# The scaled systems of the 32-row inversion kept in two PSUM banks

## What is computed

```python
def step(S, inputs):
    q_t, k_t, v_t, g_t, b_t = inputs
    S = S * jnp.exp(g_t)[..., None, None]
    kv = jnp.einsum('bhk,bhkv->bhv', k_t, S)
    u = b_t[..., None] * (v_t - kv)
    S = S + jnp.einsum('bhk,bhv->bhkv', k_t, u)
    o_t = jnp.einsum('bhk,bhkv->bhv', q_t * scale, S)
    return (S, o_t)
...
up_w = ste_sign(up_weight)
down_w = ste_sign(down_weight)
hidden = jnp.einsum('bsd,hd->bsh', x, up_w) * up_scale
hidden = jax.nn.relu(hidden)
out = jnp.einsum('bsh,dh->bsd', hidden, down_w) * down_scale
```

## Time and profile before

| | |
|---|---|
| time, median of 3 runs | 1524.98 us (1524.01 to 1525.74) |
| the profiled execution, its time | 1525.26 us |
| its span, first to last instruction | 1523.5 us |
| PE busy | 1365.2 us, 90% of the span |
| DVE busy | 1120.9 us, 74% |
| ACT busy | 724.5 us, 48% |
| POOL busy | 517.7 us, 34% |
| granted TensorE clock, mean | 0.975 |
| chain that ended last, DVE L1728 | 3% of the span |
| the same, DVE L1730, L1736, L1747 | 1% each |

### The profile page before, as it was taken

The page is one execution under the profiler, slowest core; times in us unless marked ns, Lnnn a source line. Parts: engine busy times, 40 slices in busy tenths (PEclk is TensorE's granted clock), DMA queues, the critical chain, the costliest instruction groups (busy, mean ns, idle before and its releaser), DMA issues. The chain is left out here.

```text
span 1523.5 us, 24300 instructions
## 1 busy us (share of the span) xinstructions
PE 1365.2 (90%) x8972; PEld 662.7 (43%) x8972; DVE 1120.9 (74%) x1880; ACT 724.5 (48%) x1277; POOL 517.7 (34%) x426
## 2 busy tenths in 40 slices
PE   5878899999999999999798889988899888998887
PEld 2322333333333333333354366543765437654375
DVE  6878977787878777888367956769567785586854
ACT  4664666566655665665554222641225412264121
POOL 2599821022102210222145331452314523155231
PEclk9988999999999999999999999999999999999999
DMA  6420000100010001005502030020310203102121
GB/s 219 159 77 2 6 8 5 34 25 5 10 34 26 5 10 33 26 1 206 190 22 53 6 79 29 15 54 19 66 36 8 53 21 63 36 7 54 27 31 42
DMA packets 79573, 68.51 MB, mean 45 GB/s; under 512 B 45952, under 2 KB 67168, under 8 KB 76896
## 3 DMA queue, kind: packets, MB, share of 16 engines
q1 hardware_dynamic: 79456, 66.96, 14.9%
HBM read 44.87 MB, written 17.87 MB: 41 GB/s over the span
## 5 line engine op out<-in xcount | busy, mean ns | idle before, releaser
L599 DVE TENSOR_REDUCE mS<-bank 128x1 f16<-128x512 f32 x512 | 328.8, 684 | 123.6 <-PE bank L1105 121.7
L917 ACT ACTIVATE probs<-bank 128x512 f16<-128x512 f32 x512 | 277.2, 595 | 163.3 <-PE bank L1112 163.1
L1159 PE MATMUL bank<-rows,both 128*128 128x512 f16 x1024 | 242.9, 380 | 1.1 <-DVE th L628 1.1
L408 POOL TENSOR_TENSOR h<-th,h 128x512 f16<-128x512 f32 x58 | 68.0, 1172 | 235.4 <-ACT h L888 235.4
L2099 PE MATMUL fbank<-both,hid 128*128 128x512 f16 x512 | 122.9, 403 | 24.6 <-DVE hid L1646 24.6
L1159 PEld LDWEIGHTS bank<-rows,both 128*128 128x128 f16 x1024 | 91.4, 98 | 122.3 <-issue 15.8
L2083 PE MATMUL fbank<-rows,both 128*128 128x512 f16 x512 | 118.4, 385 | 4.7 <-ACT hid L1904 4.7
L2067 PE MATMUL abank<-rows,both 128*128 128x512 f16 (+1 forms) x480 | 113.0, 387 | 5.7 <-PEq L149 5.7
L1105 PE MATMUL bank<-qk 32*128 32x512 f16 x512 | 100.7, 388 | 18.6 <-DVE mS L599 8.6
L1112 PE MATMUL bank<-qv,qk 32*128 32x512 f16 x512 | 100.1, 388 | 0.0
L1173 PE MATMUL bank<-dn,h 128*128 128x512 f16 x256 | 98.4, 384 | 0.0
(11 more groups left out here) (292 smaller groups left out, 2658.2 us busy)
## 6 DMA issues: line engine op xcount, KB each, us to landing
h<-in_ug SPq DMA_DIRECT2D x8, 1024.0 KB, 5.0
lt_scratch<-big SPq DMA_DIRECT2D x16, 384.0 KB, 2.7
dn<-in_down SPq DMA_DIRECT2D x2, 2048.0 KB, 11.2
x_scratch<-th SPq DMA_DIRECT2D x16, 256.0 KB, 2.1
res<-x_scratch SPq DMA_DIRECT2D x16, 256.0 KB, 3.6
out_x<-res SPq DMA_DIRECT2D x16, 256.0 KB, 2.0
both<-in_w SPq DMA_DIRECT2D x2, 1548.0 KB, 10.1
t_scratch<-tok SPq DMA_DIRECT2D x8, 384.0 KB, 3.6
```

The source lines that it names most:

```text
L408: pool.tensor_tensor(h16(ft, 1), row32, h16(ft, 0), ALU.subtract).then_inc(S["row_lo"], 1)
L599: v.tensor_reduce(mS[:, u % 2, qt, 32 * j + DH:32 * j + DH + 1], SA[n % 2][:, :], AX.X, ALU.max).then_inc(S["max_done"], 1)
L917: a.activation(probs[:, n % (2 * G), :], SB[n % 2][:, :], ACT.Exp, scale=float(DH) ** -0.5).then_inc(S["p_ready"], 1)
L1159: mm = pe.matmul(GB[n % 2][:, :], w[:, kt, col:col + P], xnb(b, kt), start=r == 0, stop=r == 2 * KT - 1)
```

## The change

Two of the three banks `vbank` become one tensor `vpair` of 2 x 512 words per partition. As `lsp`, 32 rows of 32 words, it holds the scaled systems: L1722 now reads `lsys` and `ssol` in SBUF and writes `lsp`. L1728 and L1736 read their second operand from `lsp`, L1741 writes `half` there, L1747 reads it there. `lsys` itself keeps only what was loaded. `t_t`, `prod` and `t_n` stay in SBUF. DVE waits, ahead of L1722, until the last KQ filling has been taken. The sequence of instructions on every engine, their shapes and their counts are the same as before. In the changed kernel the lines of the inversion stand two (up to L1721) or three lines lower (from L1722 on).

```diff
-        vbank = [ctx.enter_context(nc.psum_tensor(f"vbank{i}", [P, 512], F32)) for i in range(3)]
+        vpair = ctx.enter_context(nc.psum_tensor("vpair", [P, 2, 512], F32))
+        vbank = [vpair[:, 0], vpair[:, 1], ctx.enter_context(nc.psum_tensor("vbank2", [P, 512], F32))]
...
         t_n = prod
+        lsp = vpair[0:TT * SYS].rearrange("p b (a c) -> p (b a) c", c=BS)
...
-                    v.tensor_tensor(lsys, lsys, ssol[:, :].rearrange("p (j i) -> p j i", j=1).to_broadcast([TT * SYS, BS, BS]),
+                    v.wait_ge(S["v_took"], VI[b, "KQ", TT - 1, 1] + 1)
+                    v.tensor_tensor(lsp, lsys, ssol[:, :].rearrange("p (j i) -> p j i", j=1).to_broadcast([TT * SYS, BS, BS]),
                                     ALU.mult).then_inc(S["ls_r"], 1)
...
-                        v.tensor_tensor(block3(2, i, i), diagonal(t_t, i, False), diagonal(lsys, i, True), ALU.mult).then_inc(S["sub"], 1)
+                        v.tensor_tensor(block3(2, i, i), diagonal(t_t, i, False), diagonal(lsp, i, True), ALU.mult).then_inc(S["sub"], 1)
...
-                    half = lsys[:, HB:BS, 0:HB]
+                    half = lsp[:, HB:BS, 0:HB]
...
-                                        lsys[:, c:HB, HB:BS].rearrange("p z (x y) -> p x y z", x=1).to_broadcast([TT * SYS, SLICE, HB, w]),
+                                        lsp[:, c:HB, HB:BS].rearrange("p z (x y) -> p x y z", x=1).to_broadcast([TT * SYS, SLICE, HB, w]),
```

## The result

The changed kernel takes 1491.23 us (median of 4 runs, 1488.51 to 1492.37) against 1525.36 us of the kernel before (4 runs, 1524.01 to 1526.44). The ratio is 0.9774, with a 95% interval of 0.9757 to 0.9791: faster, by 34 us. The forecast was 1486.4, in a range of 1484 to 1501. In two later comparisons the same kernel had ratios of 0.9748 (0.9723 to 0.9773) and 0.9758 (0.9741 to 0.9774), with medians of 1487.60 and 1489.49 us.

A forecast was written before the change was run, and what follows sets the result against it. The four inversions on DVE were taken to bound the kernel. Removed holding by POOL (24.5 us) and the step (14.4), limited by PE's room, cut 38.9 us: 1525.3 - 38.9 = 1486.4 us, range 1484 to 1501.

The forecast's parts named there:

- What bounds: The four inversions, 155 us in all on DVE alone; cuts there come off the end until something else is late.
- Held by POOL: In L1728, DVE waits while POOL reads SBUF; a PSUM operand removes all of it, 24.5 us.
- third rival: DVE is still held by POOL through its SBUF operand; only 14.4 us gained, 1510.8 us, chance 0.06.
- The step at 1.04 ns per element: L1728 and L1736 read 32-word steps in PSUM at 1.04 ns, not 1.77; 3.61 us per inversion, 14.4 in all.
- first rival: In L1728 and L1736, a step costs in PSUM what it costs in SBUF; 1500.8 us, chance 0.16.
- Fixed cost of PSUM: For the inversion's 23 readers of a PSUM operand, 2 ns each, taken as nothing.
- The inversions: Cuts of 10.14, 10.15, 9.80 and 8.84 us; held against the room on PE, together 38.9 us.
- The cover on PE: PE's down projection ahead of L2243 lets the first block loop come forward at most 10.08 us, without PE pausing.
- The sum: Whole kernel: 1525.3 - 38.9 = 1486.4 us, with transfers, POOL, block loop and next batch's start shifting along.
- the forecast's own range: Total time from 1484.4 us, all room on PE used, to 1490.1 us, PSUM writes at the slow rate.
- second rival: Every PSUM reader in the inversions pays 51 ns fixed cost, 4.7 us in all; 1491.1 us, chance 0.05.
- the estimate of 1492: Total time if each of 23 PSUM readers pays 65 ns more, taking back 1.5 us per inversion.

The follow-up runs named there:

- Experiment 1: Kernel before, with POOL writing zeros in place of subtracting from the sixth hidden tile on: 1499.02 us, ratio 0.9825.
- Experiment 2: Changed kernel, with POOL writing zeros in place of subtracting from the sixth hidden tile on: 1487.07 us, ratio 0.9742.
- experiment 3: Kernel before, with the scaling writing the systems turned into an idle SBUF tile, so L1728 and L1736 read along rows: 1519.28 us, ratio 0.9953.
- Experiment 4: Changed kernel without the last four products and sums of the inversion, leaving each inverse's upper right quarter zero: 1485.70 us, ratio 0.9739.
- Experiment 5: Changed kernel with scale_down(0) moved from the middle of the inversion to behind its last copy: 1511.43 us, ratio 0.9903.
- Experiment 7: Second run of the changed kernel with the inverse's lower right quarter copied into the banks and read there by L1750: 1484.59 us, ratio 0.9743.
- the execution of 1498.16 us: Profiled execution of the unchanged changed kernel in the first of its two later comparisons, whose median was 1487.60 us: 1498.16 us.

## Why the prediction was right

**What bounds: right.** The inversion lay on the path whole. The chain of the changed kernel is the same with shorter pieces. The forecast did not see one thing: in the second batch of the kernel before, PE ends the down projection at 1073.41 and the block loop starts at 1073.42, so there PE was already as late as POOL.

**Held by POOL, 24.5 us: right in size and cause.** Experiment 1 gave 24.2 us in L1728 without touching the products. Experiment 2 shows that the PSUM operand takes away all of it, which leaves the third rival nothing. The forecast's evidence against that rival was thinner than it says: of the 128 instances of L1713 and L615, 70 overlap a POOL instruction and only 33 start with more than 0.2 us of one still to run; none of these was held. The scaling, put down as unchanged, is held for another 0.2 us per batch as before.

**The step at 1.04 ns per element, 14.4 us: right.** The first rival, with 1500.8 us, fell with the 620 ns for 450 elements: a step of 32 words costs nothing in PSUM. The Trainium skill's rule on neighbours, "Advanced Engine Details and Errata", section PSUM Cachelines, does not carry over from matmuls to these DVE reads. That the step, and not two SBUF operands, makes the slow rate is shown from both sides: experiment 3 with two SBUF operands and no step is at full rate, L1750 with one PSUM operand and a step in SBUF is slow. L1747 (L1750 in the changed kernel) was left at its old length, and stayed there (20.11 and 20.05 us in all).

**Fixed cost of PSUM, nothing: right within what counts.** 2 elements take 152 to 153 ns with a bank as operand, 157 ns for the same product with both operands in SBUF (experiment 1), and the reduction of 2 in SBUF 153. By the errata table of "VectorE: DVE Perf Modes" in the Trainium skill, an estimate would have 65 ns more on each of 23 readers; the 153 ns against 157 ns do not agree with it. Writing costs 8 ns per instruction, 0.04 us per inversion.

**The inversions: 38.6 us, forecast 38.9.** 155.15 us became 116.57. The 0.35 missing are the scaling (5.88 in place of 5.83), 0.04 us per inversion in L1731, the 8 ns of each of L1744's writes, and gaps.

**The cover on PE: right, and it mattered.** Forecast: 10.08 us of room in the first batch, a start of L1646 at 854.0, no pause, the end at 874.39. Measured: 854.72, no pause, 874.86, with the whole first inversion 0.53 us later than before. The forecast had the path shorter by 38.87 us; it is 38.5. The slow tile after the pause, 9.74 us against 6.99, is 39% more and not the 44% of the forecast; nothing was built on that figure. Experiments 4 and 5 show both sides of it: beyond this room nothing is to be had, and without the cover a third of the gain in time is left.

**The sum: 2.1 us short in the profiled execution, 4.8 in the median.** This is the one step that missed, "transfers, POOL, the block loop and the next batch's start follow in the same order and shift with it". They did follow, but not at the same length. The stretches outside became 1.2 us longer (492.3 to 493.5), and what lies ahead of the first inversion 0.5 us (834.97 to 835.50); 38.5 - 1.2 - 0.5 = 36.8. From the profiled execution to the median of 1491.2 are 2.7 us more, and the other three runs show clocks of 0.978 to 0.980 where this one shows 0.984. The sum had no term for what the clock does elsewhere, and the median lies 1.1 us outside the forecast's own range of 1484.4 to 1490.1. It is inside the stated range because that was stretched to take in the first rival, which is a piece of luck; the later medians, 1487.60 and 1489.49, lie in the own range. The time alone would have spoken for the second rival (1491.1), and for the estimate of 1492 that the forecast made by the table of "VectorE: DVE Perf Modes" in the Trainium skill: it is the 153 ns of the 2-element product, in place of 200, that rules them out. Whether the change itself moves the clock's low stretches is open. Of the kernel before, all runs in the comparisons of experiments 5 and 7 lie at 0.971 to 0.978, of the changed kernel at 0.973 to 0.986. Most of that is PE's pause, which is gone: the inversions had clocks of 0.91, 0.96, 0.96 and 0.91 and now have 1.00, by an estimate from these rows (0.09 x 39.37 + 0.04 x 39.31 + 0.04 x 38.63 + 0.09 x 37.84 us) 10 us of clock missing in a span of 1523.5, or 0.007 of the 0.009 between the two profiled executions. The rest is not explained.

## What to carry to other kernels

When a small product on DVE with two SBUF operands lasts a microsecond, look at what POOL reads in the same moment, and compare the line's own undisturbed forms; one operand in PSUM ended it here, and a chain of dozens of small products gains more by that than by fewer elements. An fp32 operand that DVE reads in steps of 32 words belongs in PSUM if a bank is free for the time (1.04 against 1.77 ns per element here; other steps were not tried). Before claiming the whole of a cut, add up what the next engine has queued ahead of the point where it joins, and keep the instructions that release that engine inside the shortened stretch.

## What was not expected

A DVE write to a bank costs 8 ns more than one to SBUF (L1744 against L1755, 16 instances each), for which the forecast had kept 3.7 us in its range. The scaling, with two SBUF inputs, is held for half a microsecond (1747 against 1231 ns) by POOL's instruction of 835.00 to 836.16, and for 0.9 us (2152 ns) in the execution of 1498.16 us. The holding goes both ways: POOL's next subtraction starts at 836.30 inside the scaling, which ends at 837.24, and takes 1.95 us in place of 1.15. POOL's 64 subtractions take 80.7 us in all before and 80.6 after, so the change took nothing from them. A pause of PE does not always cost the same: after 3.87 to 3.89 us the next 32 products took 9.88, 8.48, 8.77 and 9.52 us in the four batches of experiment 3, and after 4.45 us 9.74, 8.77, 8.52 and 9.99 in the kernel before, in place of 7.0; after pauses of 0.58 to 1.46 us in experiment 3 they took 7.08. And the same stage of the same kernel can spend more of its time at the lower clock level from one execution to the next: 0.90 against 0.99 over the last 75 us, 4.8 us.
